# Narrow products of two layers from rounded halves, in the last stage of a four-layer kernel

## The reference

```
# layer 0: attention over 512 cached keys and the sequence's own 32 (32 query heads, 8 key heads, width 128)
q = rope(rmsnorm(x @ Wq.T)); k = rope(rmsnorm(x @ Wk.T)); v = x @ Wv.T
x = x + softmax(q @ k_all.T * scale, masked) @ v_all @ Wo.T

# layer 1: a full product, and a mixture of 8 experts of rank 16, of which each token takes two
base   = x @ W.T                                   # 512 -> 512
logits = x @ Wr.T + 5.0 * one_hot(language)        # 512 -> 8
gates  = softmax of the two largest logits, 0 elsewhere
h      = x @ A.T                                   # 512 -> 8 * 16
x = x + base + 2.0 * (h * gates) @ B

# layer 2: a full product with a bias, and a rank-16 adapter that each sequence names
x = x + x @ W.T + b + 2.0 * (x @ lora_A[slot]) @ lora_B[slot]

# layer 3: a rank-16 adapter alone
x = x + (x @ B[slot]) @ A[slot]
```

## Time and profile before

| what | us |
|---|---|
| median of 3 runs | 2354.17 |
| lowest and highest | 2353.62, 2356.63 |
| the profiled execution, its own time | 2350.98 |
| its span in the trace | 2349.1 |
| TensorE busy | 2317.4 (99%) |
| VectorE busy | 1489.8 (63%) |
| ScalarE busy | 1357.4 (58%) |
| GpSimd busy | 509.1 (22%) |

### The profile page before, as it was taken

The page is one execution under the profiler, slowest core; times in us unless marked ns, Lnnn a source line. Parts: engine busy times, 40 slices in busy tenths (PEclk is TensorE's granted clock), DMA queues, the critical chain, the costliest instruction groups (busy, mean ns, idle before and its releaser), DMA issues.

```text
span 2349.1 us, 48514 instructions
## 1 busy us (share of the span) xinstructions
PE 2317.4 (99%) x14320; PEld 1997.8 (85%) x14320; DVE 1489.8 (63%) x4154; ACT 1357.4 (58%) x4300; POOL 509.1 (22%) x538
## 2 busy tenths in 40 slices
PE   8999999998999999999999999999999999999998
PEld 6887777777898888899999999999998888888886
DVE  5899999983666666666666666666665344334333
ACT  4888888864666666666666666666665222222221
POOL 5211121211223333332222222222223111111101
PEclk9999999998999999999999999999999999999999
DMA  5344454448988989899999898999996333333331
GB/s 205 92 126 114 110 130 113 112 118 308 356 285 285 286 280 291 280 293 288 293 292 289 289 290 288 287 297 292 289 291 206 96 101 94 102 99 105 98 97 47
DMA packets 400358, 488.62 MB, mean 208 GB/s; under 512 B 63136, under 2 KB 334752, under 8 KB 397216
## 3 DMA queue, kind: packets, MB, share of 16 engines
q1 hardware_dynamic: 363296, 351.93, 49.0%
q0 software_dynamic: 36864, 134.23, 17.3%
HBM read 397.89 MB, written 88.08 MB: 207 GB/s over the span
## 4 chain that ended last, share of the span: by engine, by line
PE 71%; DVE 20%; issue 6%; SPq 1%; DMA 1%; DVEq 1%; ACT 0%; ACTq 0%
PE s_bank L1010 18%; PE o_bank L1022 16%; PE pt L1057 8%; DVE q_t L668 5%; PE proj L1509 5%; PE proj L1511 5%; PE proj L1510 5%; DVE q_t L684 5%; DVE part_s L659 4%; DVE probs L977 2%; PE o_bank L1038 2%; PE wide L1551 1%; PE wide L1556 1%; PE slim L1540 1%; PE wide L1552 1%
## 5 line engine op out<-in xcount | busy, mean ns | idle before, releaser
L977 DVE CUSTOM_DVE_ANT_0 probs<-s_bank,mask 128x544 f32<-128x544 f32 x512 | 370.9, 724 | 437.1 <-PE s_bank L1010 317.2
L931 ACT ACTIVATE probs<-probs,neg_max 128x544 f32<-128x544 f32 x512 | 383.9, 750 | 411.1 <-DVE neg_max L977 411.1
L1010 PE MATMUL s_bank<-k_t,q_t 128*128 128x288 f32 (+1 forms) x2048 | 561.1, 397 | 11.2 <-ACT wo_early L533 5.1
L1022 PEld LDWEIGHTS o_bank<-p_t,v_c 128*128 128x128 f32 x4096 | 527.4, 192 | 29.6 <-DMA v_c<-in_v_rows,v_row 0.4
L1022 PE MATMUL o_bank<-p_t,v_c 128*128 128x128 f32 x4096 | 540.1, 275 | 0.0
L1010 PEld LDWEIGHTS s_bank<-k_t,q_t 128*128 128x128 f32 x2048 | 351.0, 191 | 73.3 <-DVE neg_max L977 10.9
L138 POOL DMA_INDIRECT v_c<-in_v_rows,v_row x256 | 255.9, 999 | 300.3 <-PE o_bank L1022 259.9
L1057 PE MATMUL pt<-ident,probs 128*128 128x128 f32 x2048 | 311.6, 275 | 0.0
L737 PE MATMUL acc<-w_hi,x_hi 128*128 128x512 f32 x764 | 304.3, 398 | 0.1
L903 ACT ACTIVATE p_t<-pt 128x512 f32<-128x512 f32 x512 | 296.1, 578 | 10.3 <-PE pt L1057 1.2
L738 PE MATMUL acc<-w_lo,x_hi 128*128 128x512 f32 x764 | 299.5, 392 | 0.0
(11 more groups left out here) (152 smaller groups left out, 3160.3 us busy)
## 6 DMA issues: line engine op xcount, KB each, us to landing
k_t<-in_k_pages SPq DMA_DIRECT2D x1024, 128.0 KB
q_spill<-wo_early SPq DMA_DIRECT2D x512, 64.0 KB, 1.8
q_t<-q_spill SPq DMA_DIRECT2D x64, 512.0 KB
o_spill<-o_t SPq DMA_DIRECT2D x64, 512.0 KB, 5.2
raw<-o_spill SPq DMA_DIRECT2D x64, 512.0 KB, 3.5
k_t<-in_w_qkv SPq DMA_DIRECT2D x11, 1024.0 KB, 5.7
v_spill<-wo_early SPq DMA_DIRECT2D x8, 1024.0 KB, 8.1
k_spill<-wo_early SPq DMA_DIRECT2D x128, 64.0 KB, 1.8
```

The lines of the kernel that those rows point to most:

```text
L931: nc.scalar.activation(probs[:, j % SLOTS_P], probs[:, j % SLOTS_P], ACT.Exp, scale=-1.0, bias=neg_max[:, j % 2:j % 2 + 1], accum_out=row_ ...
L977: nc.vector.tensor_tensor_reduce(out=probs[:, j % SLOTS_P], in0=s_run, in1=mask[:, par], scale=-SCALE, scalar=3.0e38, op0=ALU.add, op1=ALU ...
L1010: last = pe.matmul(s_bank[:, columns].rearrange("p (s t) -> p s t", t=PSIZE), q_t[:, par, g], k_t[:, par, slots, g], start=True, stop=True)
L1022: last = pe.matmul(o_of(n), v_c[:, par, c, g * HD:(g + 1) * HD], p_t[:, i, c], start=g < QUAD and c == 0, stop=False)
```

## The change

The narrow products of layers one and two are computed from float32r halves, as the wide ones are: `xt_hi` with the upper and the lower half of the narrow weights, and `xt_lo` with the upper half, twelve matmuls in the place of four float32 ones. Layer three stays as it was.

For this, ScalarE rounds `wr_a` and GpSimd subtracts its lower half once, ahead of tile 0. For `down2` both are done in each tile: ScalarE `down2_hi` after the copy of the turned tile, VectorE `down2_lo` after the halves of `low` in layer one. In layers one and two the float32 copy `x_t` is gone; VectorE subtracts `xt_hi` straight from the PSUM bank `turn`. In layer one that subtraction moves ahead of the split of chunk 1 and of the routing. The turning of `low_halves` becomes an ordinary float32r matmul with a rounded identity `ident_r`. In layer two the heads in the chain stand otherwise: three (were two) behind the transposes, none (was one) in the middle of the wide product.

```diff
@@ ScalarE @@
             def x_turn_out(t, layer):
                 act.wait_ge(x_turned, t * LAYERS + layer + 1)
-                nc.scalar.activation(x_t[:, :, :].rearrange("p c n -> p (c n)"), turn[:, :], ACT.Copy).then_inc(xt_out, 1)
-                if layer < 2:
+                if layer == 2:
+                    nc.scalar.activation(x_t[:, :, :].rearrange("p c n -> p (c n)"), turn[:, :], ACT.Copy).then_inc(xt_out, 1)
+                else:
                     nc.scalar.activation(xt_hi[:, :, :].rearrange("p c n -> p (c n)"), turn[:, :], ACT.Copy).then_inc(xt_hi_done, 1)
...
             def chain(t, ahead, beyond):
                 x_turn_out(t, 0)
+                act.wait_ge(down_in[0], (t + 1) * 16 * TB)
+                nc.scalar.activation(down2_hi[:, :, :, :], down2[:, :, :, :], ACT.Copy).then_inc(down_hi_done, 1)
                 upper_up(t, 0)
...
+            nc.scalar.activation(wr_a_hi[:, :, :], wr_a[:, :, :], ACT.Copy).then_inc(w_hi_done, 1)
             nc.scalar.activation(w1_hi[:, :, :], w1[:, :, :], ACT.Copy).then_inc(w_hi_done, 1)
             upper(1, 0)
+            nc.scalar.activation(ident_r[:, :], ident[:, :], ACT.Copy).then_inc(ident_r_done, 1)
@@ GpSimd @@
             pool.wait_ge(w_hi_done, 1)
+            nc.gpsimd.tensor_sub(wr_a_lo[:, :, :], wr_a[:, :, :], wr_a_hi[:, :, :].bitcast(F32)).then_inc(w_lo_done, 1)
+            pool.wait_ge(w_hi_done, 2)
             for c in range(DC):
@@ VectorE @@
-                nc.vector.tensor_tensor(xt_lo[:, :, :], x_t[:, :, :], xt_hi[:, :, :].bitcast(F32), ALU.subtract)\
+                nc.vector.tensor_tensor(xt_lo[:, :, :], turn[:, :].rearrange("p (c n) -> p c n", n=P),
+                                        xt_hi[:, :, :].bitcast(F32), ALU.subtract)\
                     .then_inc(xt_lo_done, 1)
...
                 if before:
                     result(t - 1)
+                lower_x(t, 0)
                 if ahead:
                     lower(t + 1, 1)
...
                 link(nc.vector.tensor_copy(top_f[:, :], top_i[:, :]))
-                lower_x(t, 0)
                 dve.wait_ge(ratio_done, t + 1)
...
                 halve_low(t, 0)
+                dve.wait_ge(down_hi_done, t + 1)
+                nc.vector.tensor_tensor(down2_lo[:, :, :, :], down2[:, :, :, :], down2_hi[:, :, :, :].bitcast(F32),
+                                        ALU.subtract).then_inc(down_split, 1)
                 if ahead:
                     lower(t + 1, 2)
@@ TensorE @@
-                    fill((3, 2, 2)[layer])
-                    pe.wait_ge(xt_out, t * LAYERS + layer + 1)
...
-                    for c in range(DC):
-                        if layer == 0:
-                            last = pe.matmul(slim[:, 0:E + ER], x_t[:, c], wr_a[:, c], start=c == 0, stop=c == DC - 1)
...
-                    if layer < 2:
+                    fill((3, 3, 2)[layer])
+                    if layer == 2:
...
+                    else:
                         w_hi, w_lo = ((w1_hi, w1_lo), (w2_hi, w2_lo))[layer]
...
+                            pe.wait_ge(down_split, t + 1)
+                            narrow = slim[:, 0:LOWS]
+                            down = [(down2_hi[:, :, c, :], down2_lo[:, :, c, :]) for c in range(DC)]
                         pe.wait_ge(xt_hi_done, t * 2 + layer + 1)
+                        for c in range(DC):
+                            pe.matmul(narrow, xt_hi[:, c], down[c][0], start=c == 0, stop=False)
+                            pe.matmul(narrow, xt_hi[:, c], down[c][1], start=False, stop=False)
+                        pe.wait_ge(xt_lo_done, t * 2 + layer + 1)
+                        for c in range(DC):
+                            last = pe.matmul(narrow, xt_lo[:, c], down[c][0], start=False, stop=c == DC - 1)
+                        last.then_inc(slim_done, 1)
                         for c in range(DC):
                             pe.matmul(wide[:, :], xt_hi[:, c], w_hi[:, c], start=c == 0, stop=False)
                             pe.matmul(wide[:, :], xt_hi[:, c], w_lo[:, c], start=False, stop=False)
-                        fill((2, 1)[layer])
-                        pe.wait_ge(xt_lo_done, t * 2 + layer + 1)
+                        fill((2, 0)[layer])
...
-                        last = pe.transpose(turn[:, i * P:(i + 1) * P], low_halves[:, i * P:(i + 1) * P].bitcast(F32), ident[:, :])
+                        last = pe.matmul(turn[:, i * P:(i + 1) * P], low_halves[:, i * P:(i + 1) * P], ident_r[:, :],
+                                         start=True, stop=True)
```

40 lines of the change are left out of this document (24 added, 16 removed).

## The result

| what | before | after |
|---|---|---|
| median of 10 runs each, us | 2353.14 | 2362.55 |
| lowest and highest, us | 2350.72, 2357.16 | 2359.92, 2365.4 |
| the profiled execution, its own time, us | 2350.98 | 2361.33 |
| its span, us | 2349.1 | 2359.5 |

The changed kernel is slower. The ratio of the times is 1.0038 (95% interval 1.0028 to 1.0048), about +9 us; in the two profiled executions it is +10.4 us.

A forecast was written before the change was run, and what follows sets the result against it. TensorE was taken to bound the last stage: 16 x (0.46 + 0.44) = 14.4, last tile +0.42 - 0.15, together +14.7 us on 2350.98; plus 3.19, 2368.9 us. Own range 2363 to 2375 (63%); 8 in 10: 2351 to 2399.

The forecast's parts named there:

- TensorE bounds the stage: Last stage: TensorE busy 508.01 of 509.42 us, so work added to its queue counts in full, sixteen times.
- The load of 128 x 128 weights sets the step of a narrow float32r matmul: Narrow products: each record pays its own weight load, a step of 0.111 to 0.116 us.
- Rival 1: Narrow float32r matmuls: width does not help, wholly or in part, steps up to 0.231 us; 2398 or 2421 us; chance 15%.
- rival 2: Narrow matmuls: cheaper loads, step near 0.06 us, -9 us, 2345; between 0.06 and 0.09 within 0.2%; chance 11%.
- Layer two +0.44 a tile: Layer two's 64-wide narrow product on TensorE: twelve records at 0.111 us instead of 0.89 us, +0.44 us.
- Layer one +0.46 a tile: Layer one's 136-wide narrow product on TensorE: twelve records at 0.116 us instead of 0.93 us, +0.46 us.
- The turning costs nothing: Turning `low_halves` on TensorE: four transposes a tile become float32r matmuls, 0.11 to 0.111 us; bounds -0.05 to +0.12 each.
- The order costs nothing in the middle tiles: TensorE's queue: heads are moved, not added, 32 a tile as before, with no wait for `xt_lo`.
- I count these as even: Tile 0: the 0.53 us wait for `xt_lo` goes, but the routing starts later behind a slow split.
- A tile takes 34.9 us: Sign of being right: a tile takes 34.9 us in the changed profile, before 34.0, without TensorE waits in middle tiles.
- rival 3: Last stage: added work falls into TensorE's idle time, hiding 1 or 2 us; with step near 0.09, +2, 2356; chance 8%.
- The last tile: Last tile: layer two at half clock, +0.86 instead of +0.44 us; layer one's routing 0.15 shorter on balance.

The follow-up runs named there:

- second probe: Changed kernel plus groups of 12 float32r matmuls, each behind 48 of 512 columns, once ahead of tile 0; steps 0.112 us from 16 to 192 columns.
- first probe: Changed kernel plus groups of 16 float32r and float32 matmuls of different shapes, once ahead of tile 0; first 16-wide group 0.112 us a record, then 0.213.

## Why the prediction was right, and where its sum was off

Point by point:

- **TensorE bounds the stage, and whatever is added to its queue counts in full, sixteen times: right for the thirteen tiles without a wait.** In them sixteen more records cost 1.80 us a tile, eight fewer give 0.88. In tile 0, tile 13 and the last tile TensorE waits for another engine, and there it failed; see below.
- **The load of 128 x 128 weights sets the step of a narrow float32r matmul: right, and shown.** The step is 0.1116 at 64 and at 136 columns, 0.112 from 16 to 192 in the second probe, and it halves with the stationary columns, the only thing in the rows that the load goes by. Rival 1 (width doesn't help) would have needed 0.231, and rival 2 (cheap loads) 0.06; both are out. The shorter record of a transpose's load (139 ns) was no hint of a cheaper step.
- **Layer two +0.44 a tile: measured +0.45.**
- **Layer one +0.46 a tile: measured +0.41.** The prediction took the old step of 0.116, "the rows with the same stationary operand and the same width". But 0.116 was the streaming of a float32 record, 136 x 0.85 ns, just above the load. The float32r record streams in 0.061 by the same text, so its step had to be the floor, 0.111. The text had both numbers and took the wrong one. The error is 12 x 0.005 = 0.05 us a tile.
- **The turning costs nothing: right** to 0.01 us for the pair and for the single ones. The part alone even gives 0.10 a tile, only partly explained. In the changed kernel the step in front of layer two's transposes is 0.24 us where it was 0.28. This -0.04 was not in the sum.
- **The order costs nothing in the middle tiles: right** (34.00 against 34.01). For tile 0 the prediction wrote "I count these as even", and that failed: the order alone costs it 0.97 us. The 0.53 us wait for `xt_lo` went, as said, but with the order alone one of 1.52 us for `low_halves` came, and 0.68 of it is left in the changed kernel.
- **A tile takes 34.9 us: measured 34.82**, 0.81 more and not 0.90. The 0.05 of layer one and the 0.04 of the residual make up the difference.
- **Sixteen tiles: wrong.** Tile 13 had 0.51 us of waiting of its own before, which the longer tile takes up, so that it lost 0.17 and not 0.8. The sum multiplied by 16 what was read from one tile. The totals of the earlier trace rows showed 1.41 us of idle time in 15 tiles, and rival 3 named them; the forecast itself left them out. (Rival 3's own price of +2 us doesn't follow either: at a step of 0.09 the sum is 24 x 0.09 - 1.82 = 0.34 us a tile, 5.4 in all, and less 1.41 it is +4. And the 0.11 for a faster kernel is rival 2 whole, not rival 2 less its weak edge.)
- **The last tile: wrong by more than a microsecond.** The sum gives it +0.90 + 0.42 - 0.15 = +1.17; it has +0.05. Layer two is nearly as said, +0.76 against +0.86. Layer one has -0.58, where the prediction had -0.15 + 0.46 = +0.31. Its narrow product lies in the chain of waits, and so does the routing: counted from the tile's start, the logits come 0.42 us later (2.59 before, 3.01 after), but from there to the turning of `low_halves` it is 3.40 us where it was 4.39. `xt_lo` has left this piece (0.69), and the subtraction for `gap` took 0.56 us before and 0.16 after. Why that one instruction was so long before no run shows. Layer three has -0.13 (8.43 to 8.30), at nearly the same granted clock (0.73 and 0.75). Since the clock's fall can move such a tile by 2 us from profile to profile, only the gain in layer one, where the clock is 1.00 in both, can be relied on.
- **Ahead of tile 0, nothing:** no wait for the lower halves of the weights is to be seen there, as said.

The sum was +14.7 us, the profiles show +10.4 and the runs about +9 (6.6 to 11.3 by the interval). What failed is the sum's size and not its mechanism: the terms for layer one, tile 0, tile 13 and the last tile. Of the 4.3 us between forecast and profiles, 1.3 lie in tiles 1 to 12 and 14, 0.7 in tile 13, 1.1 in the last tile, and 1.2 are the stage's earlier start. Tile 0 has +0.98 where the forecast had 0.90, and that is luck: the order was counted at nothing, and the narrow product of layer one in full, though it falls into the wait. The forecast's median lies another 2.0 us off because it added 3.19 us, the distance between the median of three runs before and the profiled one; for the changed kernel that distance is 1.22. The median lies in the range, half a microsecond below the forecast's "own range".

## What to carry to other kernels

When TensorE bounds a stage, count a narrow product by its loads of stationary columns, not by its passes or its multiplications: on 128 stationary columns twelve narrow float32r matmuls in the place of eight float32 records lose, and the way to win was to make the narrow operand the stationary one. Here that needed float32r (0.77 us for a product of 64 columns, 0.89 before, 1.34 in the changed kernel); in float32 the exchange cost 1.23. Other types were not tried. Read the step of a record as the larger of two numbers, its load and its streaming, and take the load once the streaming falls below it. Before a product is rearranged, look at what stands in the other engines' queues ahead of the residual: here one 0.31 us copy, or a fetch in smaller pieces, in the wrong place ate the gain.

## What the runs showed of the hardware

- A matmul of type float32r on 128 stationary columns takes 0.112 us from 16 to 192 moving columns, 0.120 at 256, 0.147 at 320, 0.173 at 384 and 0.229 at 512. On 64 stationary columns it takes 0.058 us at 64 moving columns and 0.060 at 128, and on 32 stationary ones 0.032.
- In the first probe a run of narrow matmuls, with TensorE shown busy all the time, went with a fall of the granted clock from 1.00 to 0.50 (1.2 GHz), and in the wide groups behind it the clock was at 1.00 again. In the kernel itself, where a narrow group of twelve stands between wide ones, it stayed at 1.00. Whoever measures a narrow matmul by itself has to read the granted clock beside it.
- A float32 group with 64 stationary columns between float32r heads cost 0.36 us beyond its records, at both of its edges. Neither the type nor the number of columns does it alone: a float32 group on 128 stationary columns took 0.89 us for eight records of 0.111 in the kernel before, and a float32r group on 64 took 0.77 for twelve of 0.060. Why the two together cost more stays open.
- An eight-column instruction of VectorE (`lang_bias`) took 0.22 us in one order of work and 1.25 in another, beside the same GpSimd subtraction, which went from 1.27 to 2.09.
- A fetch in pieces of 64 bytes took SyncE 0.55 us to issue, one of the same data in pieces of 256 bytes 0.35.
